# A diffusion step without a mixing matrix per batch: POOL's matrix work goes, ACT scales x and makes a bracket, DVE scales and adds in one instruction

## The reference

```python
# 1 diffusion, per batch: reflecting second differences along d and along s
x = x + zX * lap_x(x) + zY * lap_y(x) + zR * x * (1 - x)
# 2 experts: 8 gated ones and a shared one, D=128, F=512
g, u = x @ Wg[e], x @ Wu[e]
x = x + (1-sg) * sum_e p[b,e] * ((silu(g) * u) @ Wd[e]) + sg * shared
# 3 low rank terms by language:  x = x + (x @ A[l].T) @ B[l].T + emb[l]
# 4 attention of 16 heads of 8, keys from x, queries and own values from a side input, then Wo
```

## Time and profile before

| | us |
|---|---|
| median of 3 executions | 480.68 |
| lowest, highest | 477.71, 484.77 |
| the profiled execution, own time | 480.29 |
| span of its profile, first to last instruction | 478.5 |
| mean granted clock of PE | 0.959 of full |

### The profile page before, as it was taken

The page is one execution under the profiler, slowest core; times in us unless marked ns, Lnnn a source line. Parts: engine busy times, 40 slices in busy tenths (PEclk is TensorE's granted clock), DMA queues, the critical chain, the costliest instruction groups (busy, mean ns, idle before and its releaser), DMA issues.

```text
span 478.5 us, 7727 instructions
## 1 busy us (share of the span) xinstructions
PE 435.6 (91%) x2278; PEld 328.0 (69%) x2278; DVE 338.5 (71%) x578; ACT 273.9 (57%) x544; POOL 203.4 (43%) x245
## 2 busy tenths in 40 slices
PE   5889889779999999999999999999999978888886
PEld 2668677658778787777778877688788554455453
DVE  5587467596777688767767886776688658557763
ACT  2548547646554655565556645465555646657674
POOL 4556667784322363233226432233577424224340
PEclk9789979989999999999999999999999979879999
DMA  5423423400002010000110100001220814665630
GB/s 158 123 75 103 119 67 85 133 26 23 2 0 67 23 39 29 22 0 0 34 54 13 52 0 1 0 13 55 67 66 17 184 39 127 171 155 129 165 104 22
DMA packets 27890, 30.68 MB, mean 64 GB/s; under 512 B 4276, under 2 KB 22296, under 8 KB 27864
## 3 DMA queue, kind: packets, MB, share of 16 engines
q1 hardware_dynamic: 26664, 29.99, 22.4%
q0 software_dynamic: 768, 0.28, 0.3%
q10 hardware_dynamic: 432, 0.10, 0.1%
HBM read 22.73 MB, written 7.35 MB: 63 GB/s over the span
## 4 chain that ended last, share of the span: by engine, by line
PE 57%; DVE 13%; issue 8%; DMA 8%; ACT 6%; POOL 5%; SPq 1%; POOLq 0%; DVEq 0%; ACTq 0%
PE acc_ps L522 6%; PE g_ps L522 5%; PE g_ps L524 5%; PE g_ps L523 5%; DVE act_lo L1091 5%; PE acc_ps L524 5%; PE acc_ps L523 5%; PE u_ps L522 4%; PE u_ps L524 4%; PE u_ps L523 4%; DVE act_p L1087 4%; DMA w_raw<-in_L_cond_Wu 4%; DMA q_blocks<-max_rows 3%; ACT act_p L820 2%; PE pv_ps L700 1%
## 5 line engine op out<-in xcount | busy, mean ns | idle before, releaser
L820 ACT ACTIVATE act_p<-g_ps 128x512 f32<-128x512 f32 x144 | 86.1, 598 | 134.3 <-PE g_ps L524 119.7
L1087 DVE TENSOR_TENSOR act_p<-act_p,u_ps 128x512 f32<-128x512 f32 x144 | 98.5, 684 | 73.6 <-PE u_ps L524 47.0
L1091 DVE TENSOR_TENSOR act_lo<-act_p,act_hi 128x512 fp32r<-128x512 f32 x144 | 119.6, 830 | 0.2 <-ACT act_hi L825 0.2
L1299 POOL TENSOR_TENSOR xg_lo<-xg,xg_hi 128x512 fp32r<-128x512 f32 x35 | 50.7, 1449 | 146.7 <-ACT xg_hi L830 146.7
L825 ACT ACTIVATE act_hi<-act_p 128x512 fp32r<-128x512 f32 x144 | 89.8, 624 | 5.6 <-DVE act_p L1087 5.5
L522 PE MATMUL acc_ps<-act_hi,w_split 128*128 128x512 f32 x144 | 62.0, 431 | 16.4 <-DVE act_lo L1091 16.3
L522 PE MATMUL g_ps<-x_hi,w_split 128*128 128x512 f32 (+1 forms) x144 | 58.6, 407 | 1.4 <-DVE x_lo L1117 1.4
L523 PE MATMUL g_ps<-x_lo,w_split 128*128 128x512 f32 (+1 forms) x144 | 57.5, 399 | 0.0
L524 PE MATMUL g_ps<-x_hi,w_split 128*128 128x512 f32 (+1 forms) x144 | 57.4, 398 | 0.0
L524 PE MATMUL acc_ps<-act_hi,w_split 128*128 128x512 f32 x144 | 57.0, 396 | 0.0
L523 PE MATMUL acc_ps<-act_lo,w_split 128*128 128x512 f32 x144 | 56.9, 395 | 0.0
(11 more groups left out here) (184 smaller groups left out, 697.4 us busy)
## 6 DMA issues: line engine op xcount, KB each, us to landing
k_blocks<-k_rows SPq DMA_DIRECT2D x32, 96.0 KB
q_plain<-q_rows SPq DMA_DIRECT2D x8, 384.0 KB
q_blocks<-q_rows SPq DMA_DIRECT2D x32, 96.0 KB
k_plain<-k_rows SPq DMA_DIRECT2D x8, 384.0 KB
w_raw<-in_L_cond_Wg SPq DMA_DIRECT2D x8, 256.0 KB, 2.7
w_raw<-in_L_cond_Wu SPq DMA_DIRECT2D x8, 256.0 KB, 2.8
w_raw<-in_L_cond_Wd SPq DMA_DIRECT2D x8, 256.0 KB, 2.8
q_rows<-rows_hi SPq DMA_DIRECT2D x16, 128.0 KB
```

Of the source, the lines that this page charges most:

```text
L820: activation(act_p[k % 3][:], g_ps[k % 3][:], ACT.Silu).then_inc(silu_done, 1)
L1087: tt(act_p[k % 3][:], act_p[k % 3][:], u_ps[k % 3][:], ALU.mult).then_inc(prod_done, 1)
L1091: tt(act_lo[k % 3][:], act_p[k % 3][:], act_hi[k % 3][:].bitcast(F32), ALU.subtract).then_inc(act_lo_done, 1)
L1299: tt(xg_lo[e % 3][:], xg[:].rearrange("p b s -> p (b s)"), xg_hi[e % 3][:].bitcast(F32), ALU.subtract)\
```

## The change

The local terms are bracketed: x (1 - 2 zX + zR - zR x) + zX (sum of neighbours) + zY lap_y. The z tile gets two more rows, row 3 is 1 - 2 zX + zR, row 4 is -zR.

- POOL's three matrix instructions per tile go. It only copies the five z rows of the next tile's four batches into `z_now` (`pick_z`, 128x20, an addition of zero), after expert 5 in the loop and 6 slots ahead in tile 0.
- ACT, instead of one square, makes the bracket `dif_b = row4 * x + row3` per batch (four instructions of 128x128 with scale and bias from a tile) and `x_z = zY * x` per batch (four with a scale from a tile), two instructions in each of four slots (25 to 28).
- DVE: neighbours' sum and edges as before, then `dif_b * x` (128x512), then per batch `dif_a * zX + dif_b` in one instruction (four of 128x128, two in each of two slots).
- PE: per batch `x_z` times the one Laplace matrix, and `dif_a` times the identity, with a wait for each.
- At the start DVE makes the low part of the first weight part instead of POOL; ACT's second weight part comes behind the first rounding; PE has one more product on zeros behind the diffusion. The first side load no longer waits for `mix`.

```diff
-MIX_AHEAD, SQUARE_AHEAD = 6, 4
+PICK_AHEAD, SCALE_AHEAD = 6, 5
...
-        z_all = sb("z_all", [128, 3, B])
+        z_all = sb("z_all", [128, 5, B])
+        z_now = sb("z_now", [128, 5, TB])
+        zero = sb("zero", [128, 1])
...
-                else:
-                    sp.wait_ge(mix_ready, 1)
                 sp.dma_start(side_in[:], blockwise(a["fside_BxSxS_0"][batches(f)])).then_inc(side_loaded, 16)
...
             def diffuse(f):
-                pe.wait_ge(dif_ready, f + 1)
-                pe.wait_ge(mix_ready, f + 1)
                 for b in range(TB):
-                    dst = aux_ps[:, b * S:(b + 1) * S]
-                    mm(dst, dif_a[:, b], ident, start=True, stop=False)
-                    last = mm(dst, x_in[:, b], mix[:, b], start=False, stop=True)
+                    pe.wait_ge(x_z_ready, f * TB + b + 1)
+                    mm(aux_ps[:, b * S:(b + 1) * S], x_z[:, b], lap_t, start=True, stop=False)
+                    pe.wait_ge(dif_ready, f * TB + b + 1)
+                    last = mm(aux_ps[:, b * S:(b + 1) * S], dif_a[:, b], ident, start=False, stop=True)
                 last.then_inc(aux_written, 1)
...
             pe.wait_ge(squares_loaded, 16)
             diffuse(0)
+            mm(g_ps[0][:], act_p[0][:, 0:128], act_p[0][:], start=True, stop=True)
             pe.wait_ge(first_split, 1)
...
-            def square(f):
-
-                act.wait_ge(x_loaded, f * 16 + 16)
-                if not isinstance(f, int) or f:
-                    act.wait_ge(dif_ready, f)
-                activation(dif_b[:], x_in[:], ACT.Square).then_inc(squared, 1)
-
-            square(0)
+            def scale_x(f, part):
+
+                z = z_all[:, :, 0:TB] if isinstance(f, int) and f == 0 else z_now
+                if part == 0:
+                    act.wait_ge(x_loaded, f * 16 + 16)
+                    if not isinstance(f, int) or f:
+                        act.wait_ge(dif_ready, f * TB)
+                        act.wait_ge(z_picked, f)
+                    else:
+                        act.wait_ge(z_ready, 2)
+                for b in (part % 2 * 2, part % 2 * 2 + 1):
+                    if part < 2:
+                        activation(dif_b[:, b], x_in[:, b], ACT.Identity, scale=z[:, 4, b:b + 1], bias=z[:, 3, b:b + 1])\
+                            .then_inc(bent, 1)
+                    else:
+                        activation(x_z[:, b], x_in[:, b], ACT.Identity, scale=z[:, 1, b:b + 1]).then_inc(x_z_ready, 1)
+
+            for part in range(4):
+                scale_x(0, part)
             split_part(0)
-            split_part(1)
             act.wait_ge(aux_written, 1)
             activation(x1_hi[:, 0], aux_ps[:], ACT.Identity).then_inc(aux_rounded, 1)
+            split_part(1)
             round_xg(0, 0)
...
                 elif part == 1:
-                    dve.wait_ge(dif_step, f * 4 + 2)
-                    tt(dif_a[:], dif_a[:], over_s(z[:, 0]), ALU.mult).then_inc(dif_step, 1)
-                elif part == 2:
-                    dve.wait_ge(squared, f + 1)
-                    tt(dif_b[:], dif_b[:], over_s(z[:, 2]), ALU.mult).then_inc(dif_step, 1)
+                    dve.wait_ge(bent, f * TB + TB)
+                    tt(dif_b[:], dif_b[:], x[:], ALU.mult).then_inc(dif_step, 1)
                 else:
-                    dve.wait_ge(dif_step, f * 4 + 4)
-                    tt(dif_a[:], dif_a[:], dif_b[:], ALU.subtract).then_inc(dif_ready, 1)
+                    if part == 2:
+                        dve.wait_ge(dif_step, f * 3 + 3)
+                    for b in (part % 2 * 2, part % 2 * 2 + 1):
+                        stt(dif_a[:, b], dif_a[:, b], z[:, 0, b:b + 1], dif_b[:, b], ALU.mult, ALU.add).then_inc(dif_ready, 1)
...
             nc.vector.memset(minus_one[:], -1.0)
+            nc.vector.memset(zero[:], 0.0).then_inc(warm_set, 1)
...
-            ts(z_own[:], z_all[:, 0], -2.0, 1.0, ALU.mult, ALU.add).then_inc(z_step, 1)
-            diffuse_part(0, 0)
+            ts(z_all[:, 3], z_all[:, 0], -2.0, 1.0, ALU.mult, ALU.add).then_inc(z_step, 1)
+            ts(z_all[:, 4], z_all[:, 2], -1.0, None, ALU.mult).then_inc(z_ready, 1)
             dve.wait_ge(z_step, 1)
-            tt(z_own[:], z_own[:], z_all[:, 2], ALU.add).then_inc(z_ready, 1)
-            for part in range(1, 4):
+            tt(z_all[:, 3], z_all[:, 3], z_all[:, 2], ALU.add).then_inc(z_ready, 1)
+            for part in range(4):
                 diffuse_part(0, part)
...
+            dve.wait_ge(w_hi_done, 1)
+            tt(w_lo[:, 0, 0], w_raw[0][:], w_hi[:, 0, 0].bitcast(F32), ALU.subtract).then_inc(w_lo_done, 1)
             dve.wait_ge(aux_rounded, 1)
...
-            def make_mix(f, part):
...
+            def pick_z(f):
+
+                pool.wait_ge(aux_written, aux_of("diffuse", f - 1) + 1)
+                tt(z_now[:], z_all[:, :, batches(f)], zero[:].unsqueeze(2).to_broadcast([128, 5, TB]), ALU.add).then_inc(z_picked, 1)
...
-            pool.wait_ge(squares_loaded, 16)
-            pool.wait_ge(z_loaded, 16)
-            for part in range(3):
-                make_mix(0, part)
-            split_part(0)
+            pool.wait_ge(w_lo_done, 1)
             split_part(1)
```

More of the change, by code:

```diff
@@ L865, in _ @@
                     round_projections()
-                for kind, f, b in first_at(k + SQUARE_AHEAD):
-                    if kind == "diffuse":
-                        square(f)
+                for part in range(4):
+                    for kind, f, b in first_at(k + SCALE_AHEAD - part):
+                        if kind == "diffuse":
+                            scale_x(f, part)
             def copy_max(b, n):
@@ L899, in slots @@
                     if not isinstance(t, int):
-                        for kind, f, b in next_at(k + SQUARE_AHEAD, t + 1):
-                            if kind == "diffuse":
-                                square(f)
+                        for part in range(4):
+                            for kind, f, b in next_at(k + SCALE_AHEAD - part, t + 1):
+                                if kind == "diffuse":
+                                    scale_x(f, part)
             with act.Fori(1, NT - 1) as t:
@@ L990, in diffuse_part @@
                 x = x_in
-                z = z_all[:, :, batches(f)]
+                z = z_all[:, :, 0:TB] if isinstance(f, int) and f == 0 else z_now
                 if part == 0:
@@ L1325, in _ @@
                         multiply_self(f, b)
-                for part in range(3):
-                    for kind, f, b in first_at(k + MIX_AHEAD - part):
-                        if kind == "diffuse":
-                            make_mix(f, part)
+                for kind, f, b in first_at(k + PICK_AHEAD):
+                    if kind == "diffuse":
+                        pick_z(f)
             with pool.Fori(1, NT - 1) as t:
@@ L1337, in _ @@
                         multiply_self(t + 1, PROD_AFTER[e, "split"])
-                    if e == MIX_AFTER:
-                        for part in range(3):
-                            make_mix(t + 1, part)
+                    if e == PICK_AFTER:
+                        pick_z(t + 1)
             for e in range(NE):
```

29 lines of the change are left out of this document (8 added, 21 removed).

## The result

The changed kernel takes 472.36 us (median of 4 runs, 470.43 to 474.13) against 480.18 of the kernel before (4 runs, 477.71 to 484.77): ratio 0.985, 95% interval 0.980 to 0.990. That is 7.8 us by the medians and 7.2 by the ratio. Forecast were 471.0 and a gain of 9.7, range 466.5 to 477.5. The gain is under the two per cent that the prediction took as the border: by its own count this is "the same", to which it had given 0.56. The profiled execution has 470.62 us and a span of 468.8.

A forecast was written before the change was run, and what follows sets the result against it. PE bounds the middle; the start waits on POOL's mix chain at half clock, and DVE bounds diffusion preparation. 5.7 + 3.0 + 1.0 = 9.7 us off 480.29 gives 470.6, or 471.0 against the 480.68 median; range 466.5 to 477.5.

The forecast's parts named there:

- Start: Before the first products: shorter chain and PE clock held up together give 5.7 us, bounds 2.0 to 6.5.
- The chain: At the start: without POOL's mix building, the first gate product comes at 11.9 instead of 15.88, 4.0 us earlier.
- The clock: At the start: PE's higher clock level holds, so the nine gate products save another 1.7 us.
- End of the first tile: DVE-bound stretch preparing the next diffusion: less DVE work and POOL contention give 3.0 us, bounds 1.2 to 4.4.
- 3.45: First tile's end: DVE time in us for the new diffusion instructions, against 6.0 before, 2.6 less.
- 0.4 more from low parts that POOL lengthened: First tile's end: DVE's low parts get shorter once POOL's matrix instructions go, 0.4 us on top of 2.6.
- What is added and costs nothing: ACT's 2.6 us of brackets and scaled x, mostly covered by its idle time; if not, 0.75 us over three tiles.
- Tiles 1 and 2: Diffusions inside the loop: shorter last DVE work and earlier PE start give 0.5 us per tile, 1.0 in all.
- B: Rival: only the start pays, POOL's other work bringing first-tile PE gaps back; 475.0 us, chance 0.23.
- C: Rival: the clock falls at the start all the same, PE working only in pieces; 474.7 us, chance 0.12.
- D: Rival: the earlier start also moves DVE's small setup work off POOL's; 467.3 us, chance 0.13.
- E: Rival: POOL instructions hold each short DVE instruction in tiles 1 to 3; 483.0 us, chance 0.05.

The follow-up runs named there:

- no extra product: Changed kernel without the extra warming product on zeros behind the first diffusion; 471.72 us in one run.
- casts and masks late: Changed kernel with DVE's casts, language selection and masks moved from slot 2 to slots 8 and 10; 472.98 us, 0.985 of the kernel before.
- all small work apart: Changed kernel with DVE's projection low parts moved from slot 2 to slot 6, casts and masks to 10 and 12; 471.25 us, 0.981 of before.
- later tiles only: Kernel before with its old start, but the diffusions of tiles 1 to 3 made the new way; 477.55 us, 0.999 of before.
- wide instructions: Changed kernel with two 128x512 DVE instructions instead of four short fused ones in tiles 1 to 3; 473.17 us in one run.
- start-only: Changed kernel with only tile 0's diffusion made the new way, tiles 1 to 3 as before; 473.65 us, 0.990 of the kernel before.
- ACT's parts sooner: Changed kernel with ACT's four parts in slots 21 to 24 instead of 25 to 28; 472.57 us, 0.982 of the kernel before.
- stores spread: Changed kernel with tile 0's six query-row stores issued one per slot behind that slot's weight load; 464.26 and 463.32 us in two sets.

## Why the prediction was right, and which term was not

- **Start, 5.7 forecast, 5.4 measured** (5.6 in the second profile). The chain gave 4.1 of the 4.0 forecast. The clock gave 1.6 of 1.7, read at the first up product, 13.96 against 19.66; at the first down product 0.3 of it is spent again, since PE waits 1.18 us for DVE's low part there instead of 0.88. ACT's pointer operands cost what the bias row had promised. DVE's short instruction took 0.34 us, 0.07 more than the row with an immediate scalar, and the next followed after 0.27 instead of 0.20; PE was behind after the first, so that didn't matter. The rule of half throughput that the prediction took from the Trainium skill ("Vector Engine (DVE) Microarchitecture Reference", section "Points that are easy to get wrong") would have made it about 0.40 with the immediate and more with the pointer, by the prediction's estimate: the measured 0.34 doesn't bear it out.
- **End of the first tile, 3.0 forecast, 1.0 measured** (0.7 in the second profile). This is the term that was mis-sized, and it is most of the difference between 9.7 and 7.8. Three parts of it failed. First, the DVE cost "3.45" of the new diffusion: from start to next start it took 1.68 + 0.07 + 0.60 + 1.31 + 0.73 = 4.4 us, and 5.4 in the second profile, where before it was 6.0; POOL stood beside one pair of short ones, in the second profile beside both. Second, "0.4 more from low parts that POOL lengthened": the four low parts in this stretch took 4.0 us before, and 4.4 and 5.6 after. I took contention away where POOL's `mix` had stood and left the other POOL work where it was, but it moved. Third, the brackets stood under "What is added and costs nothing", and they hold up xg's rounding, so that xg's split meets the low part: 0.8 us from the rounding of the late weight part to the down product. From the down product at 95.79 (91.00) to the diffusion 2.0 us were won, and 1.0 was lost before it; in the second profile 0.84 and 0.16.
  How much is left also hangs on the clock. From ACT's rounding of the late part to tile 1's diffusion it took 16.2 to 16.5 us in the three profiles with the old parts. With the new ones it took 15.25 in the first profile of the changed kernel, where the clock was at the lower level for 3.4 us behind the gap, and 16.4 in the second, where it was there for 6.7. The other variants fall into the same two groups: 15.3 to 15.4 with 3.4 us at the lower level (no extra product, casts and masks late, all small work apart), 16.3 and 16.5 with 6.7 us or a little more (later tiles only, wide instructions). So with the shorter fall about 1 us is won there, and with the longer one nothing. With the old parts the length made no difference (3.4 us in two profiles, 7.0 in the start-only one). What decides the length of the fall is open.
- **Tiles 1 and 2, 1.0 forecast, 1.3 measured** (0.6 and 0.7). The wait of 0.60 for `dif_a` is gone, and the one of 0.6 a slot before is as it was. What is left up to 8.3, 0.4 us between the first down product and the first large gap and 0.2 in tile 3, no term of the prediction had.
- **The rivals.** B (only the start) would have been 475.0; the start-only kernel is at 473.65, and the intervals of the start-only and the changed kernel overlap, so the times don't rule B out. What speaks against it is in the traces: the third gap of tile 0 (2.26, and 1.35 in the start-only kernel) is gone, and so is the wait for `dif_a` in tiles 1 and 2. C fell: the grant was 1.00. D didn't come: the gap in slot 2 was 1.80 instead of 1.98, in the same place, since POOL's work moved along with DVE's. Behind it the clock stayed up in the first profile after (1.00 over 24 to 36) and fell in the second (0.86), as it had before. E fell as a sum, but not as a mechanism: one short instruction in tile 0 was held for 1.12 us, in the second profile the longest took 1.37, and in tiles 1 and 2 none was held (0.60 for every pair).

## What to carry to other kernels

When an engine that shares something with another is relieved, its other work moves: ask where that work lands, and not only where the old one stood. Ask the same of work that is "hidden" on a third engine: two brackets on ACT decided here which of two instructions came first. A queue that issues stores ahead of a load that somebody waits for makes that load late; here the six stores in front of a load, twice in tile 0, cost about as much as the whole change gave, or more (8 to 9.5 us by the medians). And where PE waits at the start, products on zeros kept its clock up; too many of them stand in the way of the first real product, as with nine of them here.

## What the runs showed of the hardware that I had not expected

- The attention stage, which is the same in all these kernels, took from 99.5 to 105.9 us in the 14 profiles. Up to the end of tile 3 two executions of one kernel lay close twice (368.91 and 369.23, 359.43 and 359.56). So much of the spread of the times is made in that stage, but not all: the start-only profile lost its time before it.
- After a gap of 1.79 or 1.80 us at about 23.7 us the clock fell in some executions (0.86 to 0.88 over 24 to 36 in the second profile of the changed kernel, in the start-only one and in that with ACT's parts sooner) and stayed at 1.00 in others (the first profile, both with the stores spread, those with wide instructions and without the extra product).
- A load of 256 KB issued behind six stores of 128 KB landed after 8.4 us, where the median of these loads is 2.7 to 2.9 us.
- A DVE instruction of 128x128 with two SBUF tiles takes 0.27 us with an immediate scalar, 0.34 with one from a tile, and 1.1 to 1.4 when a POOL instruction stands beside it. So four short ones aren't hit four times: the pair of 1.39 us has one instruction of 1.12, and the other took its usual 0.34.
